# A Mamba layer between two mixing layers: the product by C of eight scan steps moved to GpSimd, with another order of steps

## What is computed

```python
x = x + 0.5 * ffn(layernorm(x))        # time mixing with the token before, sigmoid(r) * (relu(k)**2 @ Wv)
x = x + mamba(layernorm(x))
x = x + 0.5 * ffn(layernorm(x))        # the same weights again
```

```python
h = exp(delta * A[d, n]) * h + delta * B[n] * xc      # decay * h + dbx
y = sum over n of h * C[n]
```

## Time and profile before

| | us |
|---|---|
| median of 3 runs | 4943.83 (4943.6 to 4944.37) |
| the profiled execution, its own time | 4949.61 |
| its span, first to last instruction | 4947.8 |
| mean granted TensorE clock | 0.958 |

### The profile page before, as it was taken

How to read it: one execution, slowest core, us unless ns; L and a number is a source line. 1 busy time by engine, 2 the same in 40 slices (tenths; PEclk the granted TensorE clock), 3 DMA queues, 4 the chain that set the end, 5 groups by cost and what they waited for, 6 DMA issues and landing times.

```text
span 4947.8 us, 57971 instructions
## 1 busy us (share of the span) xinstructions
PE 4318.2 (87%) x16832; PEld 2400.0 (49%) x16832; DVE 4493.3 (91%) x3650; ACT 2902.5 (59%) x6355; POOL 3206.1 (65%) x3328
## 2 busy tenths in 40 slices
PE   6777989898899989989898899989889898898787
PEld 2344545455454544545454454545545454454443
DVE  2799999999999999999999999999999999999982
ACT  2555656566665566656656665666656656665552
POOL 1666767576675767767576676767667576676761
PEclk8888999999999999999999999999999999999788
DMA  2446656555655655556555655656666565665551
GB/s 81 141 128 179 172 172 177 165 178 162 186 170 148 186 157 183 176 175 184 161 171 161 185 170 150 187 178 172 172 184 170 154 184 150 187 177 147 169 148 62
DMA packets 423053, 810.71 MB, mean 164 GB/s; under 512 B 41264, under 2 KB 41264, under 8 KB 418640
## 3 DMA queue, kind: packets, MB, share of 16 engines
q1 hardware_dynamic: 422736, 807.00, 56.4%
HBM read 772.25 MB, written 34.60 MB: 163 GB/s over the span
## 4 chain that ended last, share of the span: by engine, by line
DVE 34%; PE 20%; issue 18%; POOL 16%; ACT 6%; DMA 4%; DVEq 0%; SPq 0%; POOLq 0%; ACTq 0%
DVE decay L1086 16%; POOL dbx L1293 10%; DVE g L1094 10%; PE mm L484 5%; DMA c_all<-bc_scratch 4%; PE y_acc L568 4%; DVE xc L1032 3%; PE mm L473 3%; PE mm L532 2%; PE mm L495 2%; POOL xout L1282 1%; DVE xc L1038 1%; PE mm L510 1%; PE mm L520 1%; ACT rows L692 1%
## 5 line engine op out<-in xcount | busy, mean ns | idle before, releaser
L1293 POOL TENSOR_TENSOR dbx<-u,b_all 128x1024 f32<-128x1024 f32 x1024 | 2413.5, 2357 | 1046.2 <-DVE g L1094 1040.1
L1086 DVE TENSOR_TENSOR_SCAN decay<-decay,state,dbx 128x1024 f32<-128x1024 f32 x1024 | 2406.0, 2350 | 198.7 <-ACT decay L890 195.2
L568 PE MATMUL y_acc<-ident,g 128*128 128x128 f32 x8192 | 1139.5, 285 | 368.3 <-DVE g L1094 363.7
L568 PEld LDWEIGHTS y_acc<-ident,g 128*128 128x128 f32 x8192 | 961.5, 146 | 945.1 <-DVE g L1094 729.1
L1094 DVE TENSOR_TENSOR g<-decay,c_all 128x1024 f32<-128x1024 f32 x1024 | 1243.7, 1215 | 37.0 <-issue 25.0
L887 ACT ACTIVATE decay<-delta,neg_a 128x512 f32<-128x512 f32 x1024 | 708.6, 692 | 36.9
L890 ACT ACTIVATE decay<-delta,neg_a 128x511 f32<-128x511 f32 x1024 | 686.8, 671 | 0.0
L495 PE MATMUL mm<-wbuf_c,col 128*128 128x512 f32 x1024 | 460.8, 594 | 17.7 <-ACT delta L838 16.3
L896 ACT ACTIVATE state<-decay 128x2 f32<-128x2 f32 x1024 | 166.5, 163 | 504.0 <-DVE g L1094 502.6
L1032 DVE SCALAR_TENSOR_TENSOR xc<-mm,conv_sb,xc 128x509 f32<-128x509 f32 (+2 forms) x384 | 285.1, 742 | 51.1 <-ACT xs_last L805 42.0
L1297 POOL TENSOR_TENSOR dbx<-dbx,carry 128x1 f32<-128x1 f32 x1024 | 274.0, 268 | 80.3
(11 more groups left out here) (100 smaller groups left out, 5282.8 us busy)
## 6 DMA issues: line engine op xcount, KB each, us to landing
b_all<-bc_scratch SPq DMA_DIRECT2D x1024, 256.0 KB, 3.9
c_all<-bc_scratch SPq DMA_DIRECT2D x1024, 256.0 KB, 4.6
wbuf_d<-in_w_r SPq DMA_DIRECT2D x32, 1024.0 KB, 8.2
wbuf_c<-in_w_v SPq DMA_DIRECT2D x32, 1024.0 KB, 8.3
xin<-in_x SPq DMA_DIRECT2D x16, 1024.0 KB, 8.3
wbuf_c<-in_w_k SPq DMA_DIRECT2D x16, 1024.0 KB, 8.1
wbuf_d<-in_w_in SPq DMA_DIRECT2D x16, 1024.0 KB, 8.0
wbuf_a<-in_w_in SPq DMA_DIRECT2D x16, 1024.0 KB, 8.2
```

Source lines behind the costliest of these rows:

```text
L568: last = pe.matmul(y_acc[:, tb, j * P:(j + 1) * P], g[:, s % PAIRS, j, tb * P:(tb + 1) * P], ident[:, :], start=n == 0 and j == 0 and tb % ...
L1086: dve.tensor_tensor_scan(d, d, flat(dbx[:, s % DBX, :, :]), state[:, batch, s, 0:1], ALU.mult, ALU.add).then_inc(scan_done, 1)
L1293: pool.tensor_tensor(dbx[:, s % DBX, :, :], u[:, q % 2, :, :], b_all[:, s % BRING, :].unsqueeze(1).broadcast_to([P, QT, W]), ALU.mult).the ...
```

## The change

In the eight steps of `POOLED`, which are those of `TAPS`, the scan reads `decay` from PSUM as before but writes to `g` in SBUF, so it waits for `g` of two steps before to be summed. DVE's `weigh` and ACT's `save` are left out in these steps. POOL instead runs `pool_weigh`: it is issued behind `product` of step s+3, waits for the scan of s, copies the last column to `state`, and multiplies `g` by C in place. All who waited for `mult_done` (PE's `sum_g`, POOL's `product` for the `dbx` ring, SP's `load_c`) wait in these steps for `pool_mult_done`, and ACT may write `decay` of s+2 once the scan of s is done. On SP's queue `load_c` now comes before `load_b` in each step. Several tables have other steps, and two more `ZEROS` are added.

```diff
--- before.py
+++ after.py
@@ -132,6 +132,7 @@
+        pool_saved, pool_mult_done = sem("pool_saved"), sem("pool_mult_done")
@@ -140,29 +141,29 @@
-        SUM_SKIP = (3, 25, 33, 51)
+        SUM_SKIP = (5, 27, 35, 53)
...
-        MM_K = ((5, 7, 8, 9), (47, 48, 51, 52))
-        MM_R = ((10, 11, 12, 13), (41, 42, 44, 45))
+        MM_K = ((5, 7, 8, 9), (46, 47, 50, 51))
+        MM_R = ((10, 10, 12, 13), (41, 42, 44, 45))
...
-        ZEROS = {2: 2, 31: 2, 39: 2}
+        ZEROS = {2: 2, 31: 2, 39: 2, 30: 1, 53: 1}
...
-        RELU = ((7, 8, 9, 10), (48, 49, 52, 53))
-        TANH = ((11, 12, 13, 14), (42, 43, 45, 46))
+        RELU = ((7, 8, 9, 10), (49, 50, 53, 53))
+        TANH = ((11, 13, 14, 14), (42, 43, 45, 46))
...
-        NORM = (58, 30)
-        GATE_TANH = (28, 30, 33, 38, 59, 60, 61, 63)
+        NORM = (58, 31)
+        GATE_TANH = (28, 31, 33, 38, 59, 60, 61, 63)
@@ -172,24 +173,34 @@
-        OUT_ADD = (6, 21, 23, 25)
-        STATS = ((51, 52, 53, 54), (9, 22, 24, 27), (17, 18, 19, 20))
-        MEANS = (55, 27, 21)
+        OUT_ADD = (6, 22, 23, 25)
+        STATS = ((51, 53, 53, 54), (9, 22, 24, 27), (18, 19, 20, 21))
+        MEANS = (56, 27, 21)
...
-        MAKE_U = (-7, 10, 27, 38)
-        FFN_ADD = ((19, 20, 21, 22), (57, 58, 59, 60))
+        MAKE_U = (-8, 9, 27, 38)
+        FFN_ADD = ((18, 19, 20, 22), (57, 58, 59, 60))
...
-                38, "wv1": 39, "x": 47, "wr0": 47, "wo0": 48, "bc_out": 52, "wz1": 54, "wk0": 59, "out": 61}
+                38, "wv1": 39, "x": 47, "wr0": 47, "wo0": 48, "bc_out": 52, "wz1": 53, "wk0": 59, "out": 61}
...
-                1), "f0k": (1, 0, 1, 0), "f0r": (1, 0, 1, 0), "f0v": (1, 0, 1, 0), "mT": (1, 0, 1, 0), "z": (0, 0,
+                1), "f0k": (1, 0, 1, 0), "f0r": (1, 0, 1, 1), "f0v": (1, 0, 1, 0), "mT": (1, 0, 1, 0), "z": (0, 0,
...
+        POOLED = (29, 31, 35, 37, 39, 41, 44, 47)
...
+        def on_pool(s):
+            return s % NSTEP in POOLED
+        def so_far(it, s, pooled):
+            it, s = it + s // NSTEP, s % NSTEP
+            here = sum(q <= s for q in POOLED)
+            return it * len(POOLED) + here if pooled else it * (NSTEP - len(POOLED)) + s + 1 - here
@@ -285,6 +296,10 @@
+        def multiplied(it, s):
+            return (pool_mult_done if on_pool(s) else mult_done), so_far(it, s, on_pool(s))
@@ -332,8 +347,8 @@
-                if due(count := NSTEP * k + s - CRING + 1):
-                    sp.wait_ge(mult_done, count)
+                if due(NSTEP * k + s - CRING + 1):
+                    sp.wait_ge(*multiplied(k, s - CRING))
@@ -351,16 +366,16 @@
                 scn, front, back, ahead = has(it, 0), has(it, 1), has(it, -1), has(it, 2)
                 f, b = it + 1, it - 1
                 for s in range(NSTEP):
+                    if s + 2 < NSTEP:
+                        if scn:
+                            load_c(it, s + 2)
+                    elif front:
+                        load_c(f, s + 2 - NSTEP)
                     if s + 6 < NSTEP:
                         if scn:
                             load_b(it, s + 6)
                     elif front:
                         load_b(f, s + 6 - NSTEP)
-                    if s + 2 < NSTEP:
-                        if scn:
-                            load_c(it, s + 2)
-                    elif front:
-                        load_c(f, s + 2 - NSTEP)
                     if back and s == LOAD["wo1"]:
                         after(mark(z_pe, b, "7"))
                         sp.dma_start(wbuf["b"][:, :, :], piece(w_out, 512, 0)).then_inc(wo_loaded[1], 16)
@@ -557,7 +572,7 @@
-                pe.wait_ge(mult_done, NSTEP * it + s + 1)
+                pe.wait_ge(*multiplied(it, s))
@@ -880,7 +895,10 @@
                 q, n = divmod(s, NS)
                 if n == 0:
                     act.wait_ge(h_act.sem, h_act.at(it, f"xb{q}"))
-                if due(count := NSTEP * it + s - PAIRS + 1):
+                if on_pool(s - PAIRS):
+                    if due(count := NSTEP * it + s - PAIRS + 1):
+                        act.wait_ge(scan_done, count)
+                elif due(count := so_far(it, s - PAIRS, False)):
                     act.wait_ge(saved, count)
                 d = decay[:, s % PAIRS, :, :]
                 e = QT * q
@@ -892,7 +910,9 @@
             def save(it, s, batch):
-                act.wait_ge(mult_done, NSTEP * it + s + 1)
+                if on_pool(s):
+                    return
+                act.wait_ge(*multiplied(it, s))
                 act.activation(state[:, batch, s, :], decay[:, s % PAIRS, :, W - 1], ACT.Copy).then_inc(saved, 1)
             def body(it, bt):
@@ -1079,14 +1099,21 @@
             def scan(it, s, batch):
                 dve.wait_ge(dbx_done, 2 * (NSTEP * it + s + 1))
                 if s == 0:
-                    if due(count := NSTEP * (it - BATCHES + 1)):
+                    if due(count := so_far(it - BATCHES, NSTEP - 1, False)):
                         dve.wait_ge(saved, count)
+                    if due(count := so_far(it - BATCHES, NSTEP - 1, True)):
+                        dve.wait_ge(pool_saved, count)
                 dve.wait_ge(decay_done, 3 * (NSTEP * it + s + 1))
                 d = flat(decay[:, s % PAIRS, :, :])
-                dve.tensor_tensor_scan(d, d, flat(dbx[:, s % DBX, :, :]), state[:, batch, s, 0:1],
+                if on_pool(s) and due(count := NSTEP * it + s - PAIRS + 1):
+                    dve.wait_ge(g_summed, count)
+                o = flat(g[:, s % PAIRS, :, :]) if on_pool(s) else d
+                dve.tensor_tensor_scan(o, d, flat(dbx[:, s % DBX, :, :]), state[:, batch, s, 0:1],
                                        ALU.mult, ALU.add).then_inc(scan_done, 1)
             def weigh(it, s):
+                if on_pool(s):
+                    return
                 dve.wait_ge(scan_done, NSTEP * it + s + 1)
                 dve.wait_ge(c_loaded[s % CRING], it * (16 * NSTEP // CRING) + 16 * (s // CRING + 1))
                 if due(count := NSTEP * it + s - PAIRS + 1):
@@ -1270,8 +1297,10 @@
                 pool.wait_ge(m_dve.sem, m_dve.at(k, "silu7"))
                 pool.tensor_tensor(u[:, q % 2, :, :], delta[:, q % 2, :, :], xc2[:, QT * q:QT * q + QT, :],
                                    ALU.mult).then_inc(h_pool.sem, 1)
-                if due(count := NSTEP * (k - BATCHES + 1)):
+                if due(count := so_far(k - BATCHES, NSTEP - 1, False)):
                     pool.wait_ge(saved, count)
+                if due(count := so_far(k - BATCHES, NSTEP - 1, True)):
+                    pool.wait_ge(pool_saved, count)
                 pool.wait_ge(h_act.sem, h_act.at(k, f"lead{q}"))
                 pool.tensor_tensor(carry[:, q % 2, :], carry[:, q % 2, :], state[:, batch, NS * q:NS * q + NS, 1],
                                    ALU.mult).then_inc(h_pool.sem, 1)
@@ -1283,8 +1312,8 @@
             def product(it, s):
                 q, n = divmod(s, NS)
-                if due(count := NSTEP * it + s - DBX + 1):
-                    pool.wait_ge(mult_done, count)
+                if due(NSTEP * it + s - DBX + 1):
+                    pool.wait_ge(*multiplied(it, s - DBX))
                     pool.sem_inc(passed_pool, 1)
                 if n == 0:
                     pool.wait_ge(h_pool.sem, h_pool.at(it, f"carry{q}"))
@@ -1297,12 +1326,26 @@
                 pool.tensor_tensor(dbx[:, s % DBX, 1, 0:1], dbx[:, s % DBX, 1, 0:1], carry[:, q % 2, n:n + 1],
                                    ALU.add).then_inc(dbx_done, 1)
+            def pool_weigh(it, s, batch):
+
+                pool.wait_ge(scan_done, NSTEP * it + s + 1)
+                pool.sem_inc(passed_pool, 1)
+                states = g[:, s % PAIRS, :, :]
+                pool.tensor_copy(state[:, batch, s, :], states[:, :, W - 1]).then_inc(pool_saved, 1)
+                pool.wait_ge(pool_saved, so_far(it, s, True))
+                pool.sem_inc(passed_pool, 1)
+                pool.wait_ge(c_loaded[s % CRING], it * (16 * NSTEP // CRING) + 16 * (s // CRING + 1))
+                pool.tensor_tensor(states, states, c_all[:, s % CRING, :].unsqueeze(1).broadcast_to([P, QT, W]),
+                                   ALU.mult).then_inc(pool_mult_done, 1)
+
             def body(it, bt):
                 scn, front, back, ahead = has(it, 0), has(it, 1), has(it, -1), has(it, 2)
                 f, b = it + 1, it - 1
                 for s in range(NSTEP):
                     if scn:
                         product(it, s)
+                        if s > 2 and on_pool(s - 3):
+                            pool_weigh(it, s - 3, bt)
                     if scn:
                         for q in at(MAKE_U, s):
                             make_u(it, q, bt)
```

## The result

| | before | after |
|---|---|---|
| median of 9 runs, us | 4944.37 | 4929.2 (4926.31 to 4936.42) |
| ratio, 95% interval | | 0.997 (0.996 to 0.9981) |
| span of the profiled execution, us | 4947.8 | 4927.3 |
| mean granted TensorE clock | 0.958 | 0.967 |

What follows compares the result with a forecast made beforehand. The prediction took DVE as the bound, PE close behind, ACT and POOL able to stall it. Terms 2.4 + 0.15 - 1.7 + 0.9 + 0 - 1.0 - 1.9 = -1.15 us a chunk, x 15 = -17, gave 4927; range 4850 to 4990.

Steps and rivals of the forecast that it cites:

- 29 to 32: Steps 29 to 32, 17.75 us before: POOL's product of 29 delays head, tanh and decay; +2.4 us a chunk.
- 38 to 41: Steps 38 to 41: one product leaves (-1.13), late decay of 39 (0.7), two mixes wait (1.3); +0.9 us a chunk.
- 41 to 49: Steps 41 to 49: three products leave (-3.4), mixes or silus behind them wait for POOL (+3.4); sum 0.
- 35 to 38: Steps 35 to 38: two products leave (-2.26), late xs 3 holds taps of 37 by 0.5; -1.7 us a chunk.
- 49 to 55: Steps 49 to 55: k2 ahead of second xp delays step 51 by 3.3 us, later stalls go; -1.0 us a chunk.
- 55 to 62: Steps 55 to 62: C load first ends the product's 1.71 us wait in step 59; -1.9 us a chunk.
- The lock: VectorE mix or silu with two SBUF inputs waits until POOL's running product ends; terms 3.4 and 1.3 us a chunk.
- The tables, taken as 0: The rest: r matmul, tanhs, sum_skip, make_u, out_add and statistics move into steps with slack, zeros where PE waits; 0.
- Clock: Rival: PE's waits in steps 30 and 38 bring half clock on xs 1 and xs 4; +40 us, 4967; chance 0.30.
- No lock: Rival: both lock terms fall away in the pooled stretches; -5.85 us a chunk, -88 us, 4856; chance 0.17.
- full price: Rival: POOL in time in step 29 too, DVE's whole work leaves; -11.9 us a chunk, 4765; chance 0.08.
- Slower order: Rival: scan to SBUF slower or xp order costs more; +1 to +3 us a chunk, 4942 to 4972; chance 0.09.

Runs made afterwards that it cites:

- three of its variants: Changed kernel with old load order, 4982.06 us; with mixes and silus moved out of steps 42, 45, 48, 4923.42 us; with matmul k2 in step 51, 4929.35 us.
- the best version: Kernel before with C first, products 41, 44, 47 on POOL, mixes and silus moved, SUM_SKIP, ZEROS, NORM, GATE_TANH edited: 4858.65 us, ratio 0.9809.

## Why the prediction was right, and where not

**The total** was forecast at 4927 and is 4929.2. By stretch the sum is -1.22 us a chunk for -1.15, but it holds because errors of both signs met: -0.8 in 29 to 32, -0.4 in each of the three stretches 32 to 35, 38 to 41 and 41 to 49, +0.7 in 35 to 38, +0.9 in 49 to 55, +0.3 in 55 to 62. That the total came within 2 us is in good part luck. From the spans of the profiled executions the 20.5 us divide, one kernel behind the other, into load order -22.8 (4947.8 to 4925.0), the other tables -28.2 (to 4896.9), eight products +30.4 (to 4927.3). These spans are single executions, and that of the kernel before lay 5.8 us over its median; the ratios give -14, -39 and +38. The prediction's terms, times 15, give -28.5 for the load order (-1.9), -15 for the order of the tables (-1.0) and +26 for the stretches with pooled steps (2.4 + 0.15 - 1.7 + 0.9). The signs were right. The tables are worth about twice as much or more, the products cost more, and the load order gives less, because its 1.9 us of step 59 and its neighbours come with 0.8 lost in 35 to 38.

**What held.** *The price of a product*, 1.13 us a step, to the hundredth in steps 41, 44, 47. *The scan to SBUF*: 2338 ns for 2349, taken as 0. *POOL's load*: products and copies sum to 325.2 us (301.5 and 23.7) for 328. The page shows 302.5 more, for two reasons: instructions that overlap their neighbours by some 0.06 us count once in the busy time, and the 64 products of `make_u` (L1298) fell from 2484 to 2361 ns, which they do without pooled products too. *The lock*, 41 to 49: predicted +1.1 in each step behind, measured +1.00; the move of the mixes took it away. The Trainium skill, SBUF — State Buffer, section "SBUF: two separate sides", says the loser blocks fully. The traces agree: of the 384 mixes on `col` and silus of the changed kernel, the 243 that start while a POOL product runs all end 0.55 us behind it, however early they started; the others take about 0.74 us (mix) and 0.68 (silu). The silu's mean rose to 883 ns, just under the 900 that I had named as a sign. Of DVE's missing 78 us, mixes and silus take 63.6 (128 mixes +236 ns, 128 silus +114 ns, 64 + 64 further mixes +392 and -99 ns). *The load order*: -1.62 for -1.9, and -1.79 where it is the only edit.

**Steps 29 to 32: right cause, two details off.** The chain product, head, tanh, `decay` is as told. But POOL left the rsqrt chain earlier (`dbx` of 31 starts 0.27 us after scan 29, not 1.06), so the head starts 8.12 us after it and not 9.35: +1.6 for +2.4. And DVE's stall is not at scan 31: the gate op stayed in step 30, while only ACT's tanh moved to 31, so it stalls there 3.75 us before the product. Against the right rival, the same tables without the products, this place costs 2.28. What made POOL earlier was not tried by itself; without the products 29 to 32 is 0.66 shorter than with the old tables, and 32 to 35 is as short as in the changed kernel (13.02).

**Steps 35 to 38: the step that failed.** I took "two products leave (-2.26), but xs 3 ... holds the taps of 37 by 0.5", -1.7 in all. Among the same tables two pooled products are worth 0.34, and in the chunk that the prediction read, 14.78 us became 14.34. In chunk 8:

```profile
2664.04 2.35 DVE L1111 TENSOR_TENSOR_SCAN g<-decay,state,dbx 128x1024 f32<-128x1024 f32 x1
2666.95 2.31 DVE L1052 SCALAR_TENSOR_TENSOR xc<-mm,conv_sb,xc 128x509 f32<-128x509 f32 x3 [0.56 <-ACT xs_last L820]
2670.24 2.36 DVE L1111 TENSOR_TENSOR_SCAN decay<-decay,state,dbx 128x1024 f32<-128x1024 f32 x1 [0.98 <-ACT decay L908]
```

The taps wait 0.56, as predicted, but the next scan 0.98 more: ACT, which also waited for xs 3, starts the convolution late, and two instructions on `xin`, the head's tanh and the save stand before its `decay` of 38. I followed xs 3 to DVE's taps and not through ACT's queue. What the stretch gained in all, 0.98, is for 0.64 the tables' doing (15.35 to 14.71 without the products), where no fall of the clock is left in step 35 or 36 of the 14 chunks.

**Steps 38 to 41: near in size, by other parts.** The sum was -1.13 for the product, +0.7 for a `decay` of 39 held by the head, and +1.3 for two mixes. In chunk 8 the scan of 39 waits for nothing. One mix alone pays: in step 38 it takes 2.49 us for 0.93, in step 39 0.91 as before. -1.13 and +1.56 are +0.43; the mean is +0.51 for the +0.9 predicted.

**The tables, taken as 0.** "sum_skip ... move into steps with slack: 0" failed: `SUM_SKIP` in 35 alone is worth 13 us, and with it the clock fell behind that wait in 8 chunks and not in 14. *49 to 55* was mis-sized: step 51 loses 3.50 as told (3.3), but the later stalls give back 3.6 and not 4.3; -0.06 for -1.0. The products have no part in it (-0.12 without them). In steps 0 to 29 single steps move by up to 1.7 us, sum +0.17, and 62 to 64 give 0.16.

**The rivals.** *Clock*: in the changed kernel's profiled execution it is absent, though PE waits 2.39 us in step 30 (3.5 predicted) and 1.62 in step 38 (2.2 predicted). In three of its variants it is there, with the price of +1.5 on step 31, but not in every chunk: 7 chunks are 10 us and not 40. *No lock* and *full price* are out, by steps 42, 45, 48 and by step 30. *Slower order*: near, +0.9 in 49 to 55. Why the clock falls behind a wait of 2.4 us in some chunks and not in others of the same execution stays open; no run tells it apart.

## What to carry to other kernels

Moving work from the busiest engine pays only where its new engine is not late at that moment: price each moved instruction at its own place, by what stands behind it in the new queue, for here seven of eight together gave nothing and one cost 30 us or more. Before moving a two-input SBUF operation off VectorE, look whether GpSimd's new start meets another such operation; putting that one in the step just relieved gave 3 us a chunk, of which a later stretch took back 1.0 in one kernel and 2.4 in the other. And when a change comes with new tables, run it once with the main part switched off: that one run showed that load order and tables were the gain.

## What the runs showed of the hardware

- A mix or silu on VectorE, which reads two SBUF inputs, ended 0.55 us behind the end of the GpSimd product that it met, whenever it started: 1.92 us in the row above, 1.95 in the earlier trace rows, 2.49 in step 38, 0.91 where it met only the last 0.36 us. Free, a mix takes 0.74 us and a silu 0.68. GpSimd pays in small too, in both kernels: its column add beside such a mix took 0.52 us for 0.19.
- The scan that writes to SBUF is 11 ns shorter than the one that writes to PSUM (2338 and 2349 ns).
- The length of PE's last wait did not decide whether the clock fell. Behind 1.71 to 1.72 us in step 35 it fell in 6 of 14 chunks of the kernel before and in all 14 with the load order alone; behind 2.4 us in step 30 in 7 of 14 of one execution and in none of the changed kernel's. Falls of the granted clock in the profiled execution: 68 before, 65 with the load order alone, 47 after, 36 without the products, 33 in the best version.
